# Two FP4 feed-forward stages with the residual added on TensorE, and retention's head-masked values copied instead of multiplied

## The chip, the cores and the metric

The kernel runs as one program on one core of a Trainium2 chip. The time is device microseconds from the start to the end of one execution; the kernel before was timed three times: 1815.0, 1809.85 and 1813.59 us, median 1813.59. The engines are TensorE (PE, with its weight loads as PEld), VectorE (DVE), ScalarE (ACT), GpSimd (POOL) and SyncE (SP), which only issues DMAs. They run their own instruction streams and meet at semaphores.

## The reference, cut to what matters

```python
x = L0_attn_x                                   # 4 x 1024 tokens of 128
x = x + 0.5 * _L0_ffn_ref(_layernorm(x), ...)   # mixture of 8 experts
x = x + _L0_attn_ref(_layernorm(x), ...)        # attention, 16 heads
x = x + 0.5 * _L0_ffn_ref(_layernorm(x), ...)
x = x + 0.5 * _L1_ffn_ref(_layernorm(x), ...)   # FP4 feed-forward (touched)
x = x + _L1_attn_ref(_layernorm(x), ...)        # retention, 16 heads of 8 (touched)
x = x + 0.5 * _L1_ffn_ref(_layernorm(x), ...)   # FP4 feed-forward (touched)

def fp4_quant_dequant(x):                       # blocks of 16 along the last dim
    scale = jnp.maximum(jnp.max(jnp.abs(xb), axis=-1, keepdims=True) / 6.0, 1e-12)
    xn = xb / scale
    idx = jnp.searchsorted(_MID, jnp.abs(xn))
    q = _GRID[idx] * jnp.sign(xn) * scale       # grid 0 .5 1 1.5 2 3 4 6

def _L1_ffn_ref(x, w_gate, w_up, w_down):       # 128 -> 352 -> 128
    gate = fp4_linear(x, w_gate)                # fp4_linear rewrites both operands
    y = fp4_linear(x, w_up)
    return fp4_linear(jax.nn.silu(gate) * y, w_down)

def _L1_attn_ref(x, Wq, Wk, Wv, gn_weight, gn_bias, Wout):
    scores = jnp.einsum('bhle,bhme->bhlm', Q, K) * Dm[None] / math.sqrt(HEAD_DIM)
    out = jnp.einsum('bhlm,bhme->bhle', scores, V)   # Dm: decay mask per head
    # group norm over each head's 8 channels and 1024 tokens, then @ Wout
```

Everything is fp32 here; "FP4" means values rounded to the grid and scaled back.

## The kernel before, in words

The tokens x (128 partitions, 32 tiles of 128 channels) stay in SBUF from first to last. Eight groups of four tiles go through each feed-forward stage. The stages follow one another, and each engine has its own code for each stage, written out in order by hand: what an engine does first is what stands first in its function, whether or not its input is there. In the trace the first FP4 stage (n = 3) runs from about 1400 to 1535 us, retention from there to about 1690, the second FP4 stage (n = 5) to the end at 1818.

**An FP4 group g.** VectorE rewrites the normalised tokens to codes (lines 1309 to 1317: block maximum, scale, reciprocal, product), ScalarE makes an "anchor" of them (line 1320, a bf16 power-of-two magnitude), VectorE rounds against it twice (1323, 1324) and scales back (1359). TensorE transposes the tokens (1541), ScalarE copies the transpose out of bank 6 (1495), and TensorE multiplies by gate and up (1551) into banks 0 to 5 in two pairs of tiles. ScalarE applies SiLU to a pair (1500), VectorE multiplies it with up (1432, `products`) into the hidden values, 128 x 1408. These go the same way: VectorE codes them (`ffn_codes`), ScalarE makes the anchor (`ffn_hidden_anchor`), VectorE rounds (`ffn_hidden_round`), GpSimd scales the codes back in one instruction of 1408 elements (1475, `ffn_pool`), TensorE transposes them in three chunks of columns (1566, `hiddenT`; chunks 0 and 2 in bank 6, chunk 1 in bank 7), ScalarE copies each chunk out (1490), TensorE multiplies by down (1574) into bank 7, and VectorE adds bank 7 to x (1438, `add`). The engines work on different groups at a time: in a turn TensorE does hiddenT(g-1), gate and up of g+1, down(g-1) and the tokens of g+2. In the first FP4 stage VectorE also takes the statistics of the finished sum (256) for the next normalisation, and GpSimd finishes them (271 to 282).

**Retention.** 32 chunks of 128 tokens, eight for each sequence. For a chunk TensorE projects q, k, v into a bank (1625 to 1627), ScalarE copies it (1723) and makes four masked copies of q (1726). TensorE takes scores of four groups of heads (1633), VectorE multiplies them with the decay (1802) and q and k with their decays (1797, 1798, the `masks`), and TensorE multiplies the decayed scores by `vm` (1643): the values, four times over (index j), with all channels at zero but those of the heads with number j in each group of four. GpSimd makes `vm` (1773) as a product of the values, repeated four times, with a constant mask of ones and zeros, 512 elements. It has two buffers, and is made when the outputs of two chunks before are done.

**Between the stages.** Each engine starts retention's first steps inside the FP4 stage, at `next(lead)`: ScalarE centres, scales and copies chunks 0 to 2 there, before the transposes of group 7, and TensorE takes the first score; the rest follows group 7.

## Time and profile before

| what | value |
|---|---|
| median of three runs | 1813.59 us (1809.85 to 1815.0) |
| the profiled execution | 1820.12 us, its span 1818.2 us |
| busy over the span | PE 1652.5 (91%), DVE 1406.3 (77%), ACT 990.2 (54%), POOL 345.9 (19%) |
| a group of the first FP4 stage, 1456.30 to 1470.50 | 14.20 us: PE 11.69, DVE 13.93, ACT 8.40, POOL 5.23, clock 0.88 |
| a group of the second FP4 stage, 1750.60 to 1764.40 | 13.80 us: PE 11.36, DVE 13.28, ACT 8.19, POOL 2.62, clock 0.88 |
| retention, 1530 to 1676 | 146 us: PE 138.0, DVE 135.9, ACT 82.1, POOL 64.2, clock 0.99 |

Busy time is per engine, and the engines work side by side, so the columns do not add up to the stretch. The clock is the mean of TensorE's granted clock, 1.00 being 2.4 GHz; it has two levels, 1.2 and 2.4 GHz, so 0.88 means a part of the stretch at the lower one. An instruction's start in the timeline is counted from the span's start. "Idle before <-releaser" is the time that the engine stood idle before an instruction and the instruction that ended it. The chain that ended last is followed back from the last instruction; in retention VectorE's line 1798 is on it twice with 1.36 us, at 1603.24 and at 1639.72, and the statistics of a group (line 256) have 0.86 us busy in VectorE's timeline of the first FP4 stage.

### The profile page before, as it was taken

To read this page: it belongs to the slowest core of one execution; us is meant where nothing else is said; L and a number is where in the kernel's file an instruction comes from. 1 tells how busy PE (TensorE), PEld (TensorE's weight loads), DVE (VectorE), ACT (ScalarE), POOL (GpSimd) and SP (SyncE) were. 2 spreads that over 40 slices of the span, in tenths; PEclk is the share of its full clock that TensorE was granted. 3 is DMA by queue.
4 is the path that set the end of the run, shared out by engine and by line. 5 is a ranking of instruction groups with operands and counts; after the bars stand their busy time and mean duration, and the time that the engine had idled before them with its cause. 6 is when DMAs were issued, how large, how long until landed. Compare 5 with 4: busy or idle time off the path is not lost.

```text
span 1818.2 us, 30155 instructions
## 1 busy us (share of the span) xinstructions
PE 1652.5 (91%) x10801; PEld 962.2 (53%) x10801; DVE 1406.3 (77%) x2337; ACT 990.2 (54%) x1958; POOL 345.9 (19%) x661
## 2 busy tenths in 40 slices
PE   6899999879999999999999889999998788998686
PEld 5788888721111111111111248788887566665575
DVE  5765555688999999999999247655577897999895
ACT  3223333337888888888888752322333455654452
POOL 5311002461000001000000221011001135244211
PEclk9899999988999999999999979999999888999888
DMA  3000000121010100011101001000000000000000
GB/s 129 1 1 0 0 0 18 53 87 37 27 32 28 37 22 22 22 37 29 32 27 24 7 7 53 1 0 0 0 1 1 1 1 1 2 2 2 1 24 24
DMA packets 25301, 35.91 MB, mean 20 GB/s; under 512 B 5808, under 2 KB 19696, under 8 KB 24672
## 3 DMA queue, kind: packets, MB, share of 16 engines
q1 hardware_dynamic: 25184, 34.38, 6.3%
q8 instruction: 70, 1.15, 0.3%
q14 instruction: 47, 0.39, 0.1%
HBM read 22.57 MB, written 8.78 MB: 17 GB/s over the span
## 4 chain that ended last, share of the span: by engine, by line
PE 75%; DVE 12%; ACT 5%; issue 4%; POOL 3%; DMA 0%; SPq 0%; ACTq 0%; POOLq 0%; DVEq 0%
PE PS L968 14%; PE PS L437 12%; PE PS L956 10%; PE PS L426 7%; PE PS L427 6%; PE PS L428 6%; PE PS L945 5%; DVE neg_half L1103 3%; ACT probs L1040 3%; PE PS L1551 3%; PE PS L1633 2%; PE PS L1566 2%; POOL qk_all L1475 2%; PE PS L1643 1%; DVE qk_all L1324 1%
## 5 line engine op out<-in xcount | busy, mean ns | idle before, releaser
L1103 DVE TENSOR_REDUCE neg_half<-PS 128x2 f32<-128x1024 f32 x512 | 601.5, 1220 | 39.7 <-PE PS L945 24.8
L1040 ACT ACTIVATE probs<-PS 128x512 f32<-128x512 f32 x1024 | 529.0, 603 | 118.7 <-PE PS L956 118.4
L520 ACT ACTIVATE shared<-PS 128x512 f32<-128x512 f32 x256 | 152.7, 597 | 376.8 <-PE PS L428 364.0
L956 PE MATMUL PS<-qk_all 51*128 51x512 bf16 x1024 | 282.0, 391 | 16.9 <-ACT probs L1040 11.8
L614 DVE TENSOR_TENSOR shared<-shared,PS 128x512 f32<-128x512 f32 x256 | 174.2, 686 | 158.1 <-ACT shared L520 156.2
L968 PE MATMUL PS<-probs,Vg 128*32 128x512 f32 x2048 | 279.1, 618 | 0.0
L437 PEld LDWEIGHTS PS<-wd,shared 128*128 128x128 f32 x2048 | 250.8, 194 | 11.2 <-issue 0.5
L956 PEld LDWEIGHTS PS<-qk_all 51*128 51x128 bf16 x1024 | 71.6, 93 | 340.8 <-ACT probs L1040 321.3
L437 PE MATMUL PS<-wd,shared 128*128 128x128 f32 x2048 | 252.0, 277 | 0.0
L945 PE MATMUL PS<-qk_all 48*128 48x512 bf16 x1024 | 194.4, 392 | 17.2 <-DVE neg_half L1103 15.0
L622 DVE SCALAR_TENSOR_TENSOR x<-PS,gates,x 128x128 f32 (+1 forms) x512 | 144.1, 344 | 73.2 <-PE PS L437 73.2
L426 PE MATMUL PS<-xT_hi,wg_hi 128*128 (+1 forms) x256 | 115.7, 452 | 9.8 <-DVE shared L614 8.5
L945 PEld LDWEIGHTS PS<-qk_all 48*128 48x128 bf16 x1024 | 49.6, 94 | 137.3 <-DVE neg_half L1103 132.1
L271 POOL TENSOR_TENSOR ln_a<-stats 128x4 f32<-128x4 f32 (+2 forms) x44 | 9.7, 221 | 536.7 <-DVE stats L256 536.5
L427 PE MATMUL PS<-xT_lo,wg_hi 128*128 (+1 forms) x256 | 102.9, 402 | 0.0
L427 PE MATMUL PS<-xT_lo,wu_hi 128*128 (+1 forms) x256 | 102.8, 402 | 0.0
L428 PE MATMUL PS<-xT_hi,wg_lo 128*128 (+1 forms) x256 | 102.7, 401 | 0.0
L426 PE MATMUL PS<-xT_hi,wu_hi 128*128 (+1 forms) x256 | 102.7, 401 | 0.0
L428 PE MATMUL PS<-xT_hi,wu_lo 128*128 (+1 forms) x256 | 101.7, 397 | 0.0
L1551 PE MATMUL PS<-wguT,plane 128*128 128x352 f32 (+4 forms) x384 | 95.2, 409 | 3.0 <-ACT plane L1495 2.3
L1566 PE MATMUL PS<-ident,qk_all 128*128 128x128 f32 (+1 forms) x192 | 43.5, 398 | 46.9 <-POOL qk_all L1475 41.0
L1551 PEld LDWEIGHTS PS<-wguT,plane 128*128 128x128 f32 x384 | 69.7, 214 | 23.4 <-issue 6.7
(210 smaller groups left out, 2108.9 us busy)
## 6 DMA issues: line engine op xcount, KB each, us to landing
split<-qk_all SPq DMA_DIRECT2D x16, 384.0 KB, 3.3
qk_all<-split SPq DMA_DIRECT2D x64, 96.0 KB
qk_all<-split SPq DMA_DIRECT2D x64, 64.0 KB
qk_all<-split SPq DMA_DIRECT2D x64, 32.0 KB
shared<-OTs SPq DMA_DIRECT2D x60, 32.0 KB
probs<-in_ret_const SPq DMA_DIRECT2D x1, 1538.5 KB, 6.8
qk_all<-negT SPq DMA_DIRECT2D x96, 4.0 KB, 1.7
SC<-inverse SPq DMA_DIRECT2D x3, 512.0 KB, 5.0
```

Of the source, the lines that this page charges most:

```text
L426: pe.matmul(bank(b), lhs_hi[:, w], hi, start=True, stop=False)
L427: pe.matmul(bank(b), lhs_hi[:, w], lo, start=False, stop=False)
L428: last = pe.matmul(bank(b), lhs_lo[:, w], hi, start=False, stop=True)
L437: last = pe.matmul(bank(4 + e % 2)[:, j * P:(j + 1) * P], h[:, FCH * (e % 2) + f, j * P:(j + 1) * P], wd[:, e * FCH + f, :], start=(f == 0 ...
L520: act.activation(sg[:, f, :], bank(f), ACT.Silu).then_inc(s["silu"], 1)
L614: dve.tensor_tensor(h[:, FCH * (e % 2) + f, :], sg[:, f, :], bank(2 + f), ALU.mult).then_inc(s["h"], 1)
L945: last = pe.matmul(bank(b + strip), qs[at, slot, 0, pair, t * P:(t + 1) * P], qs[at, slot, 1, pair, half * GW:(half + 1) * GW], start=True ...
L956: pe.matmul(bank(RING_AT + use % RING), qs[rows, slot, 1, pair, kt * P:(kt + 1) * P], qs[rows, slot, 0, pair, half * GW:(half + 1) * GW], ...
L968: last = pe.matmul(bank(7)[j * 32:(j + 1) * 32, :], Vg[:, r % 2, kt, j, :], probs[:, n % 2, j, :], start=(kt == 0), stop=(kt == BT - 1))
L1040: act.activation(probs[:, n % 2, STRIPS * strip + pair, :], bank(RING_AT + use % RING), ACT.Exp, scale=ATT_SCALE).then_inc(s["exped"], 1)
L1103: dve.tensor_reduce(neg_half[m % 2][:, i % 2, :, at], bank(use_bank(i, m), 2).rearrange("p (s w) -> p s w", s=STRIPS), AX.X, ALU.max, nega ...
L1551: last = pe.matmul(bank(3 * k, 3)[:, to:to + w], xqT[:, (2 * k + j) * P:(2 * k + j + 1) * P], wguT[:, src:src + w], start=True, stop=True)
```

## The change

Five edits. (1) VectorE's `add` goes; `down` begins each tile with a matmul of x by the identity, so that the sum arises in bank 7, and ScalarE copies bank 7 over x (`added`). (2) In ScalarE's turn the anchor of the hidden codes stands before both SiLUs instead of between them. (3) GpSimd scales the hidden codes back in two instructions of 704 elements, each with its own count on the semaphore, and TensorE's `hiddenT` transposes chunks 0 and 1 for the first two tiles, then for the other two, then chunk 2. (4) `vm` is cleared once (1024 elements) and then each chunk copies only the 128 values, 4 x 4 runs of 8, to their places. (5) The waits follow these.

```diff
@@ -179,7 +179,10 @@
         rxn = carve(2 * P).rearrange("p (u w) -> p u w", u=2)
         assert taken[0] <= HW
         qd, kd = (carve(3 * P).rearrange("p (u w) -> p u w", u=3) for _ in range(2))
-        vm = carve(2 * JH * P).rearrange("p (u j w) -> p u j w", u=2, j=JH)
+        vm_at, vm = taken[0], carve(2 * JH * P).rearrange("p (u j w) -> p u j w", u=2, j=JH)
+        HEAD_STEP = P + C // (HG * JH)
+        vm_heads = [space[:, vm_at + u * JH * P:vm_at + u * JH * P + JH * HEAD_STEP].rearrange("p (j w) -> p j w", w=HEAD_STEP)
+                    [:, :, 0:P].rearrange("p j (g e) -> p j g e", g=HG)[:, :, :, 0:C // (HG * JH)] for u in range(2)]
         rtmp, state = carve(P), carve(P)
         ro, cn = carve(2 * SEQ), carve(SEQ)
         rst = carve(12).rearrange("p (a k) -> p a k", k=3)
...
@@ -1366,7 +1369,7 @@
                 dve.wait_ge(ffn["xq"], done_groups(n) + tokens)
                 link.mark(q_largest(dve, fxn[:, tokens % 2, :], tmax))
             link(q_largest(dve, hraw, amax))
-            wait(dve, ffn["hq"], c)
+            wait(dve, ffn["hq"], PAIRS * c)
             if tokens < GROUPS:
                 q_inverse(dve, link, largest_all, scale_all)
                 q_codes(dve, fxn[:, tokens % 2, :], tcode, tmax, NB_T, ffn["t_raw"])
@@ -1432,11 +1435,6 @@
                     dve.tensor_tensor(hraw[:, k * PW:(k + 1) * PW], fsg[:, k, :], bank(3 * k, 3)[:, PW:2 * PW],
                                       ALU.mult).then_inc(s["h"], 1)
 
-            def add(g):
-                dve.wait_ge(s["y"], c0 + g + 1)
-                xs = x[:, g * GT:(g + 1) * GT, :].rearrange("p t c -> p (t c)")
-                dve.tensor_tensor(xs, bank(7), xs, ALU.add).then_inc(s["added"], 1)
-
             if n == 3:
                 ffn_tokens_round(dve, link, n, 0)
             for _ in ffn_tokens(dve, link, n, 1):
@@ -1449,19 +1447,16 @@
                 if g + 2 < GROUPS:
                     ffn_tokens_round(dve, link, n, g + 2)
                 ffn_hidden_round(dve, link, n, g)
-                if g > 0:
-                    add(g - 1)
                 if n == 3 and g > 1:
                     dve.wait_ge(s["added"], c0 + g - 1)
                     ln_stats(dve, g - 2)
             if n == 3:
                 dve.wait_ge(s["added"], c0 + GROUPS - 1)
                 ln_stats(dve, GROUPS - 2)
-                dve.wait_ge(s["hq"], GROUPS)
+                dve.wait_ge(s["hq"], PAIRS * GROUPS)
             next(lead, None)
-            add(GROUPS - 1)
-            dve.wait_ge(s["added"], c0 + GROUPS)
             if n == 3:
+                dve.wait_ge(s["added"], c0 + GROUPS)
                 ln_stats(dve, GROUPS - 1)
 
         def ffn_pool(pool, n, lead=iter(())):
@@ -1472,7 +1467,11 @@
                     ln_finish(pool, 4, g - 3)
                 pool.wait_ge(s["h_code"], c + 1)
                 wait(pool, s["hT_ps"], 3 * c)
-                pool.tensor_tensor(q_blocks(hq), q_blocks(hcode), q_wide(fscale, GT * NB_I), ALU.mult).then_inc(s["hq"], 1)
+                nb = GT * NB_I // 2
+                for k in range(PAIRS):
+                    half = slice(k * PW, (k + 1) * PW)
+                    pool.tensor_tensor(q_blocks(hq[:, half]), q_blocks(hcode[:, half]), q_wide(fscale[:, k * nb:(k + 1) * nb], nb),
+                                       ALU.mult).then_inc(s["hq"], 1)
             if n == 3:
                 for g in range(GROUPS - 3, GROUPS):
                     if g == GROUPS - 1:
@@ -1498,6 +1497,11 @@
                 act.wait_ge(s["gu"], (c0 + g) * PAIRS + k + 1)
                 wait(act, s["h"], (c0 + g - 1) * PAIRS + k + 1)
                 act.activation(fsg[:, k, :], bank(3 * k, 3)[:, 0:PW], ACT.Silu).then_inc(s["silu"], 1)
+
+            def added(g):
+                act.wait_ge(s["y"], c0 + g + 1)
+                xs = x[:, g * GT:(g + 1) * GT, :].rearrange("p t c -> p (t c)")
+                act.activation(xs, bank(7), ACT.Copy).then_inc(s["added"], 1)
 
             ffn_normalise(act, n, 1)
             ffn_tokens_anchor(act, n, 0)
@@ -1516,18 +1520,20 @@
                         hiddenT(g - 1, c)
                 if g + 2 < GROUPS:
                     ffn_tokens_anchor(act, n, g + 2)
-                if g + 1 < GROUPS:
-                    silu(g + 1, 0)
                 ffn_hidden_anchor(act, n, g)
                 if g + 1 < GROUPS:
-                    silu(g + 1, 1)
+                    for k in range(PAIRS):
+                        silu(g + 1, k)
                 if g + 3 < GROUPS:
                     ffn_normalise(act, n, g + 3)
+                if g > 0:
+                    added(g - 1)
                 if g + 2 < GROUPS:
                     tokensT(g + 2)
             next(lead, None)
             for c in range(len(CHUNKS)):
                 hiddenT(GROUPS - 1, c)
+            added(GROUPS - 1)
 
         def ffn_pe(pe, n, lead=iter(())):
             s = ffn
@@ -1552,27 +1558,35 @@
                                                  wguT[:, src:src + w], start=True, stop=True)
                     last.then_inc(s["gu"], 1)
 
-            def hiddenT(r, c):
-                lo, w = CHUNKS[c]
-                pe.wait_ge(s["hq"], c0 + r + 1)
-                if c == 0:
-                    pe.wait_ge(s["xT"], c0 + min(r + 3, GROUPS))
-                    wait(pe, s["hT"], 3 * (c0 + r))
-                elif c == 1:
-                    wait(pe, s["added"], c0 + r)
-                else:
-                    pe.wait_ge(s["hT"], 3 * (c0 + r) + 1)
-                for j in range(GT):
-                    last = pe.transpose(bank(6 + c % 2)[0:w, j * P:(j + 1) * P],
-                                        hq[:, j * INNER + lo:j * INNER + lo + w], ident[:, :])
-                last.then_inc(s["hT_ps"], 1)
+            def hiddenT(r):
+
+                def turned(c, pair):
+                    lo, w = CHUNKS[c]
+                    for j in (2 * pair, 2 * pair + 1):
+                        last = pe.transpose(bank(6 + c % 2)[0:w, j * P:(j + 1) * P],
+                                            hq[:, j * INNER + lo:j * INNER + lo + w], ident[:, :])
+                    return last
+
+                pe.wait_ge(s["hq"], PAIRS * (c0 + r) + 1)
+                pe.wait_ge(s["xT"], c0 + min(r + 3, GROUPS))
+                wait(pe, s["hT"], 3 * (c0 + r))
+                turned(0, 0)
+                wait(pe, s["added"], c0 + r)
+                turned(1, 0)
+                pe.wait_ge(s["hq"], PAIRS * (c0 + r + 1))
+                turned(0, 1).then_inc(s["hT_ps"], 1)
+                turned(1, 1).then_inc(s["hT_ps"], 1)
+                pe.wait_ge(s["hT"], 3 * (c0 + r) + 1)
+                turned(2, 0)
+                turned(2, 1).then_inc(s["hT_ps"], 1)
 
             def down(r):
                 pe.wait_ge(s["hT"], 3 * (c0 + r + 1))
                 for j in range(GT):
+                    pe.matmul(bank(7)[:, j * P:(j + 1) * P], ident[:, :], x[:, r * GT + j, :], start=True, stop=False)
                     for c, (lo, w) in enumerate(CHUNKS):
                         last = pe.matmul(bank(7)[:, j * P:(j + 1) * P], hqT[0:w, c, j * P:(j + 1) * P], wdT[0:w, c, :],
-                                         start=(c == 0), stop=(c == len(CHUNKS) - 1))
+                                         start=False, stop=(c == len(CHUNKS) - 1))
                 last.then_inc(s["y"], 1)
 
             tokens(0)
...
...
@@ -1768,10 +1780,12 @@
 
             for k in range(CHUNKS_ALL):
                 b, c = k // BT, k % BT
+                if k == 0:
+                    pool.memset(vm[:, :, :, :].rearrange("p u j w -> p (u j w)"), 0.0).then_inc(s["vm_zero"], 1)
+                    pool.wait_ge(s["vm_zero"], 1)
                 pool.wait_ge(s["pj"], k + 1)
                 wait(pool, s["o_ps"], k - 1)
-                pool.tensor_tensor(vm[:, k % 2, :, :], vs[:, k % 3, :].unsqueeze(1).to_broadcast([P, JH, C]), k_col,
-                                   ALU.mult).then_inc(s["vm"], 1)
+                pool.tensor_copy(vm_heads[k % 2], vs[:, k % 3, :].rearrange("p (g j d) -> p j g d", g=HG, j=JH)).then_inc(s["vm"], 1)
                 if k == 0:
                     yield
                 if b > 0 and c == 2:
```

ScalarE's turn for one group in the middle of the second half of the first FP4 stage. Names: qk_all and shared are areas in SBUF that hold the stage's buffers, PS is PSUM; L1320 of 128x1408 is the hidden anchor, L1500 a SiLU. Before:

```order
L1490 ACTIVATE qk_all<-PS 128x512 [waits ffn_y,ffn_hT_ps] x2
L1490 ACTIVATE qk_all<-PS 96x512 [waits ffn_y,ffn_hT_ps]
L1320 ACTIVATE qk_all<-qk_all 128x512 [waits ffn_t_raw]
L1500 ACTIVATE shared<-PS 128x704 [waits ffn_h,ffn_gu]
L1320 ACTIVATE qk_all<-qk_all 128x1408 [waits ffn_h_raw]
L1500 ACTIVATE shared<-PS 128x704 [waits ffn_h,ffn_gu]
L1393 ACTIVATE xn<-x,mean 128x128 [waits ln_rstd,ffn_t_raw]
L1393 ACTIVATE xn<-x,mean 128x128 x3
L1398 ACTIVATE xn<-xn,rstd 128x128 [waits ffn_centred]
L1398 ACTIVATE xn<-xn,rstd 128x128 x3
L1495 ACTIVATE plane<-PS 128x512 [waits ffn_gu,ffn_xT_ps]
```

Now (L1323 the anchors, L1499 the SiLUs, L1504 the copy of the sum to x):

```order
L1489 ACTIVATE qk_all<-PS 128x512 [waits ffn_y,ffn_hT_ps] x2
L1489 ACTIVATE qk_all<-PS 96x512 [waits ffn_y,ffn_hT_ps]
L1323 ACTIVATE qk_all<-qk_all 128x512 [waits ffn_t_raw]
L1323 ACTIVATE qk_all<-qk_all 128x1408 [waits ffn_h_raw]
L1499 ACTIVATE shared<-PS 128x704 [waits ffn_h,ffn_gu] x2
L1396 ACTIVATE xn<-x,mean 128x128 [waits ln_rstd,ffn_t_raw]
L1396 ACTIVATE xn<-x,mean 128x128 x3
L1401 ACTIVATE xn<-xn,rstd 128x128 [waits ffn_centred]
L1401 ACTIVATE xn<-xn,rstd 128x128 x3
L1504 ACTIVATE x<-PS 128x512 [waits ffn_y]
L1494 ACTIVATE plane<-PS 128x512 [waits ffn_gu,ffn_xT_ps]
```

The hidden anchor moved in front of both SiLUs, and one copy more stands between the normalisation and the copy of the transposed tokens.

TensorE, the transposes of the hidden values of one group and the first matmul of gate and up. Before:

```order
L1566 MATMUL PS<-ident,qk_all 128x128 [waits ffn_hT,ffn_xT,ffn_hq]
L1566 MATMUL PS<-ident,qk_all 128x128 x3
L1566 MATMUL PS<-ident,qk_all 128x128 [waits ffn_added,ffn_hq]
L1566 MATMUL PS<-ident,qk_all 128x128 x3
L1566 MATMUL PS<-ident,qk_all 96x128 [waits ffn_hT,ffn_hq]
L1566 MATMUL PS<-ident,qk_all 96x128 x3
L1551 MATMUL PS<-wguT,plane 128x352 [waits ffn_h,ffn_xT]
```

Now:

```order
L1566 MATMUL PS<-ident,qk_all 128x128 [waits ffn_hT,ffn_xT,ffn_hq]
L1566 MATMUL PS<-ident,qk_all 128x128
L1566 MATMUL PS<-ident,qk_all 128x128 [waits ffn_added]
L1566 MATMUL PS<-ident,qk_all 128x128
L1566 MATMUL PS<-ident,qk_all 128x128 [waits ffn_hq]
L1566 MATMUL PS<-ident,qk_all 128x128 x3
L1566 MATMUL PS<-ident,qk_all 96x128 [waits ffn_hT]
L1566 MATMUL PS<-ident,qk_all 96x128 x3
L1557 MATMUL PS<-wguT,plane 128x352 [waits ffn_h,ffn_xT]
```

The wait for the last part of the rewrite stands behind four transposes instead of before the first. Further on, where `down` had twelve matmuls for four tiles (L1574), it now has four of x and twelve of down (L1586, L1588).

ScalarE where the first FP4 stage ends and retention begins, with the middle left out. Before (L1711 and L1715 centre and scale retention's chunks, L1719 copies a transposed chunk, L1723 and L1726 are its projection, L1490 the chunks of group 7):

```order
L1320 ACTIVATE qk_all<-qk_all 128x1408 [waits ffn_h_raw]
L1711 ACTIVATE qk_all<-x,mean 128x128 [waits ln_rstd,ld_ret]
L1711 ACTIVATE qk_all<-x,mean 128x128
L1715 ACTIVATE qk_all<-qk_all,rstd 128x128 [waits ret_centred] x2
L1719 ACTIVATE qk_all<-PS 128x128 [waits ret_xT_ps]
...
L1490 ACTIVATE qk_all<-PS 128x512 [waits ffn_y,ffn_hT_ps] x2
L1490 ACTIVATE qk_all<-PS 96x512 [waits ffn_y,ffn_hT_ps]
L1723 ACTIVATE qk_all<-PS 128x512 [waits ret_proj]
L1726 ACTIVATE qk_all<-PS,probs 128x128 x4
L1719 ACTIVATE qk_all<-PS 128x128 [waits ret_xT_ps]
```

Now (the same are L1723, L1727, L1731, L1735 and L1738, L1489):

```order
L1323 ACTIVATE qk_all<-qk_all 128x1408 [waits ffn_h_raw]
L1504 ACTIVATE x<-PS 128x512 [waits ffn_y]
L1723 ACTIVATE qk_all<-x,mean 128x128 [waits ln_rstd,ld_ret]
L1723 ACTIVATE qk_all<-x,mean 128x128
L1727 ACTIVATE qk_all<-qk_all,rstd 128x128 [waits ret_centred] x2
L1731 ACTIVATE qk_all<-PS 128x128 [waits ret_xT_ps]
...
L1489 ACTIVATE qk_all<-PS 128x512 [waits ffn_y,ffn_hT_ps] x2
L1489 ACTIVATE qk_all<-PS 96x512 [waits ffn_y,ffn_hT_ps]
L1504 ACTIVATE x<-PS 128x512 [waits ffn_y]
L1735 ACTIVATE qk_all<-PS 128x512 [waits ret_proj]
L1738 ACTIVATE qk_all<-PS,probs 128x128 x4
L1731 ACTIVATE qk_all<-PS 128x128 [waits ret_xT_ps]
```

The copy of group 6's sum stands before the first centring, and that of group 7's sum before the projection of chunk 1; each waits for its down.

## Rows read from the trace of the kernel before

**Rows 1.** Chain that ended last, 1380 to 1818: start us, us, what, count

```profile
1427.22 2.60 POOL qk_all L1475
...
1514.29 2.60 POOL qk_all L1475
...
1708.66 2.60 POOL qk_all L1475
...
1791.73 2.60 POOL qk_all L1475
```

**Rows 2.** Timeline of VectorE, 1750 to 1765: start, us, engine, line [idle before <-releaser]

```profile
1750.46 0.68 DVE L1438 TENSOR_TENSOR x<-PS,x 128x512 f32<-128x512 f32 x1
...
1751.06 1.67 DVE L1432 TENSOR_TENSOR qk_all<-shared,PS 128x704 f32<-128x704 f32 x2
...
1757.08 1.62 DVE L1317 TENSOR_TENSOR qk_all<-qk_all 128x1408 f32<-128x1408 f32 x1
...
1761.00 1.63 DVE L1323 SCALAR_TENSOR_TENSOR qk_all<-qk_all 128x1408 f32<-128x1408 bf16 x1 [0.25 <-ACT qk_all L1320]
...
1764.20 0.68 DVE L1438 TENSOR_TENSOR x<-PS,x 128x512 f32<-128x512 f32 x1
```

**Rows 3.** Groups by line and shape, 1410 to 1525: busy us, mean ns, idle before

```profile
L1323 DVE SCALAR_TENSOR_TENSOR qk_all<-qk_all 128x1408 f32<-128x1408 bf16 x8 | 13.0, 1622 | 8.8 <-ACT qk_all L1320 8.8
```

**Rows 4.** Groups by line and shape, 1690 to 1818

```profile
L1323 DVE SCALAR_TENSOR_TENSOR qk_all<-qk_all 128x1408 f32<-128x1408 bf16 x8 | 13.0, 1625 | 7.7 <-ACT qk_all L1320 7.7
```

**Rows 5.** Timeline of all engines, 1750 to 1762

```profile
1753.27 2.96 PE L1566 MATMUL PS<-ident,qk_all 128*128 128x128 f32 x12 [2.44 <-POOL qk_all L1475]
...
1756.01 5.43 PE L1551 MATMUL PS<-wguT,plane 128*128 128x352 f32 x24
...
1759.60 1.37 ACT L1320 ACTIVATE qk_all<-qk_all 128x1408 bf16<-128x1408 f32 x1
...
1761.28 2.84 PE L1574 MATMUL PS<-wdT,qk_all 128*128 128x128 f32 x24
```

**Rows 6.** Stretches: us, PE, PEld, DVE, ACT, POOL busy, clock, DMA

```profile
1754.30:1755.30 1.00, 1.00 (x6) 0.70 (x5) 0.93 (x3) 0.63 (x2) 0.00 (x0) 0.50 0.00 0
...
1427.20:1442.20 15.00, 12.34 (x64) 10.30 (x64) 12.53 (x15) 7.16 (x15) 2.59 (x1) 0.72 0.00 0
```

**Rows 7.** Timeline of all engines, 1520 to 1537

```profile
1520.12 4.91 PE L1574 MATMUL PS<-wdT,qk_all 128*128 128x128 f32 x24 [0.68 <-ACT qk_all L1490]
...
1522.96 0.68 ACT L1711 ACTIVATE qk_all<-x,mean 128x128 f32<-128x128 f32 x2
...
1535.16 0.69 DVE L1438 TENSOR_TENSOR x<-PS,x 128x512 f32<-128x512 f32 x1 [3.14 <-PE PS L1574]
...
1536.78 1.14 PE L1633 MATMUL PS<-qk_all 32*128 32x512 f32 x8
```

**Rows 8.** One line each, 1797, 1798, 1802: ns min/median/max, first and last start

```profile
L1797 DVE TENSOR_TENSOR qk_all<-qk_all,probs x32: 274/292/1358, 1529.1 to 1666.5; 128x128 f32<-128x128 f32 x32
...
L1798 DVE TENSOR_TENSOR qk_all<-qk_all,probs x32: 277/284/1364, 1529.3 to 1666.7; 128x128 f32<-128x128 f32 x32
...
L1802 DVE TENSOR_TENSOR shared<-PS,probs x128: 667/679/693, 1529.5 to 1672.9; 128x512 f32<-128x512 f32 x128
```

**Rows 9.** VectorE's groups by line and shape, 1528 to 1690

```profile
L1797 DVE TENSOR_TENSOR qk_all<-qk_all,probs 128x128 f32<-128x128 f32 x32 | 12.9, 402 | 3.2 <-ACT qk_all L1723 2.1 <-POOL qk_all L1475 0.6
...
L1798 DVE TENSOR_TENSOR qk_all<-qk_all,probs 128x128 f32<-128x128 f32 x32 | 12.3, 384 | 0.0
```

**Rows 10.** GpSimd's groups by line and shape, whole span

```profile
L1773 POOL TENSOR_TENSOR qk_all<-qk_all,probs 128x512 f32<-128x512 f32 x32 | 41.1, 1289 | 39.5 <-PE PS L1649 36.6 <-PE PS L1643 2.4
...
L1157 POOL COPY Vg<-plane 128x256 f32<-128x256 f32 x16 | 6.4, 398 | 177.9 <-PE PS L968 177.8
...
L1151 POOL MEMSET Vg<- 128x512 f32 x2 | 1.1, 547 | 0.0
```

**Rows 11.** Timeline of all engines, 1807 to 1815

```profile
1809.48 5.28 PE L1574 MATMUL PS<-wdT,qk_all 128*128 128x128 f32 x24 [0.68 <-ACT qk_all L1490]
```

8 lines of the change are left out of this document (3 added, 5 removed).

## The prediction

> **What bounds the kernel now.** I read the chain that ended last first. In both FP4 stages it repeats itself once for each of the eight groups: GpSimd's rewrite of the hidden codes (line 1475), TensorE's transposes, half of gate and up, ScalarE's anchor, VectorE's two roundings, GpSimd again. The starts of line 1475 give the length of a group [rows 1]: six periods from 1427.22 to 1514.29 in the first stage, 87.07 us or 14.5 each, and six from 1708.66 to 1791.73 in the second, 83.07 us or 13.8 each.
>
> Then VectorE's timeline of one group [rows 2]. From one add to the next are 13.74 us (1750.46 to 1764.20); 0.60 of it is the add (the products start at 1751.06), 0.25 is a wait for ScalarE's anchor (line 1320), and the rest is work. So VectorE needs 12.89 us for a group, and the chain above is level with it. The groups by line say what that wait comes to [rows 3, 4]: 8.8 us before line 1323 in the first stage, 7.7 in the second.
>
> Then all engines in the same group [rows 5]. TensorE is idle for 2.44 us before the transposes, which take 2.96 us, gate and up take 5.43, down 2.84. The anchor starts at 1759.60 although its input, the codes, is ready at 1758.70 (1757.08 + 1.62, [rows 2]), since a SiLU that waits for gate and up stands in front of it. The clock table shows 0.50, the lower level of 1.2 GHz, in the microsecond from 1754.3 [rows 6]: it falls behind TensorE's idle time in each group, for about 3 us.
>
> Last, retention. VectorE and TensorE are both nearly full there, 3.7 us per chunk at best. Lines 1797 and 1798, products of two SBUF tensors, have medians of 292 and 284 ns but maxima of 1358 and 1364, while line 1802, which has one input in PSUM, stays within 667 and 693 in all 128 [rows 8]. Each long one lies under a product of GpSimd (line 1773, 1289 ns, [rows 10]). So VectorE is held there by GpSimd.
>
> **The change, part by part.**
>
> **FP4, the add leaves VectorE.** 0.60 us a group [rows 2]. The residual goes through TensorE as four more matmuls and is copied out by ScalarE. A matmul of this shape costs 2.84 / 24 = 0.118 us at full clock [rows 5] and 5.28 / 24 = 0.22 at half [rows 11], so 0.47 to 0.88 us a group on TensorE. ScalarE's copy of a bank takes what its copies of a bank take now, 0.60; ScalarE is busy for 8.2 of 13.8 us (the table of stretches), so both have cover while the add that they replace had none. Five adds lie between the first and the last of the seven rewrites of the first stage: 5 x 0.60 = 3.0. In the second I count to the eighth rewrite: 6 x 0.60 = 3.6.
>
> **FP4, the anchor goes ahead of both SiLUs.** What it waits for is then VectorE's own codes, and its 1.37 us [rows 5] lie under the token rounds, except in the last two groups of a stage, which have no token rounds: there some 1.44 us of wait remain (1.37 and the handing over). From [rows 3, 4]: 8.8 - 2 x 1.44 = 5.9, and 7.7 - 2.9 = 4.8. What is late next: the SiLUs. They end some 11 us into a group, and the products that need them come at 12.9, so they are hidden, save before the last group of the second stage, where a group without tokens is short: I take off 0.5.
>
> **FP4, the rewrite in two halves.** GpSimd pays its fixed cost of about 0.2 us twice: half of 2.6 becomes some 1.4 us, the second half ends 0.2 us later than the whole did, but half of eight transposes is done by then. Four transposes fewer behind it are 0.5 us at full clock and 0.9 at half. This makes gate and up begin 0.3 to 1.0 us sooner, which bounds nothing while VectorE does; I count 0.
> The Trainium skill (GPSIMD Engine Reference, "Elementwise — side-by-side cycle accounting") gives a two-input instruction about 2.6 cycles an element at 1.2 GHz. By that the 1408 elements would take an estimated 3.05 us where the row shows 2.60, and the halves would give the second one 0.2 us later still; the sum would be the same.
>
> **Does TensorE's own round then bind?** Its pieces at full clock: eight transposes 0.9, the copy that bank 6 waits for 0.9 with hand-over, four transposes 0.5, gate and up 5.1, down with 28 matmuls 3.1 to 3.3, tokens 0.5, and copy and hand-over of the tokens 1.2. That is 12.2 to 12.4, just under VectorE's 12.89. With 3 us at half clock, as now, 1.5 are added: 13.8, and VectorE would gain nothing in a group of the second stage. But idle time behind the tokens shrinks from 2.44 to about 1.2 us, so I expect the fall in few groups. I take 1.5 us off for it over both stages, with 0 and 5 as ends.
>
> FP4 sum: (3.0 + 5.9) + (3.6 + 4.8 - 0.5) - 1.5 = 15.3 us gained.
>
> **Entry to retention: ScalarE's queue.** The copy of the sixth sum (group 6 of 0 to 7) stands in front of retention's first centrings, and it waits for down, which ended at 1525.0 (1520.12 + 4.91, [rows 7]). Before, the centrings ran under it (1522.96). Now copy 0.60, two centrings 0.68 and two scalings 0.68 follow down: retention's first score comes up to 2.0 us later, and the transposes of group 7 queue behind it on TensorE. The same again one step on: group 7's copy waits for its down (its old add started at 1535.16) and holds up the projection of chunk 1, 0.60 + 0.60 + 1.14 = 2.3 us with what follows, 2.0 to 2.9 with hand-over, less what stood there; so the score at 1536.78 comes 2.0 to 5.7 us later against group 6. The gain of group 7 itself is already outside my count. GpSimd's new memset of 1024 elements, some 1.0 us by twice the 547 ns for 512 [rows 10], lies beside it. I take -4.0, nearer to both delays than to one.
>
> **Retention: 128 elements copied where 512 were multiplied.** GpSimd's copy of 256 elements takes 398 ns [rows 10], so I put one of 128 at 0.3 us, with 0.25 and 0.5 as ends, against 1.29. GpSimd itself has room; what counts is VectorE held behind it. Means less medians: (402 - 292) x 32 = 3.5 us and (384 - 284) x 32 = 3.2 [rows 8, 9], 6.7 together. Other instructions of two SBUF inputs are held now and then, so I put the whole at 7 to 9 us. A copy can hold for a quarter of that time and meets a two-input instruction less often. The floor is 0 (TensorE, at 3.7 us a chunk, might bind wherever VectorE is freed), the ceiling 9. Since the stalls are in chunks where VectorE is the longer of the two, I take 6.5.
> The Trainium skill (GPSIMD Engine Reference, "Specifications") says that GpSimd's SBUF interfaces are shared with VectorE and contended by its instructions with two SBUF inputs. By that rule the copy holds VectorE too, only for less; the trace agrees for the product (1364 against 284 ns), and no copy here shows it.
>
> **The end.** Behind the last rewrite 28 matmuls at half clock follow in place of 24 [rows 11]: +0.9; the second half of the rewrite +0.2; fewer transposes behind it -0.5 to -0.9, ScalarE's copy in place of the add -0.1. That is +0.1 to +0.5 lost; I take 0.4, since TensorE idles before it and will be at half clock.
>
> **Sum.** 15.3 - 4.0 + 6.5 - 0.4 = 17.4 us gained. The profiled execution took 1820.12 us (span 1818.2), so 1802.7 for one like it. It stands 6.5 us above the median of the runs, 1813.59, and they are what the prediction is about: 1813.6 - 17.4 = 1796.2, rounded to 1796.
>
> **Rivals.**
> *TensorE's round binds.* The clock keeps falling in every group, the round stays at 13.8. For it: the transposes now come in three bursts with gaps between them, and the clock fell after 2.44 us in each group. Against: gaps shorten. FP4 then gives about 7 less (its second stage and a part of the first): 1803. Chance 0.15.
> *Retention gives nothing and the entry costs all.* TensorE, busy 138 of 146 us there (the table of stretches), binds instead. For it: in chunks of 3.7 us it has no idle time. Against: two of the long ones, at 1603.24 and 1639.72, lie on the chain that ended last (told under the table of the profile). 17.4 - 6.5 - 1.7 = 9.2: 1804. Chance 0.12.
> *Slower: the lower clock spreads from the transposes to gate, up and down.* TensorE's round is 12.3 us and half of whatever is spent at 1.2 GHz; it passes 13.8 from 3 us on, and with 8 us at half clock it is 16.3. For it: the first period, with a mean clock of 0.72, lasted 15.0 us [rows 6]; the new order breaks the transposes in two. Thirteen periods at +2.2 to +2.5 are +30, less 6.5 in retention, and with the entry about +27: 1841; with 5 us at half clock +14 - 6.5 + 4 = +12: 1825. Chance 0.05.
> *Entry and tail eat it.* Ends of all terms against me at once, within 5 us of before: 1810. Chance 0.08.
> The forecast has the remaining 0.60.
>
> **How the numbers follow.** What a measurement can tell from no change is 0.3%, 5.4 us: faster is below 1808.2. The forecast and the first two rivals are faster, 0.87, of which I leave 0.02 to slower for what I did not see; no change 0.09; slower 0.06, with 0.85 for faster. Range: all ends for me are 15.3 + 1.5 - 2.0 + 9 = 24 us, 1790, and the runs before spread by 4 below their median: 1786. Upwards it takes in both faster rivals and stops at 1808.
>
> **What would show it.** Starts of the rewrite's first half some 12.9 us apart in the second stage and 13.7 in the first, where the statistics of a group, 0.86 busy, are added; no wait at all of the hidden rounding for the anchor but in the last two groups; a granted clock of 1.00 in most of the middle groups; ScalarE's copy ahead of retention's centrings with TensorE idle behind down; lines 1797 and 1798 with means below 320 ns and a copy near 0.3 us. I am wrong if the periods stay at 13.7 in the second stage (the round of TensorE), or the chunks of retention keep their 138 us with the stalls gone.

## The result, and the profile after

Six timed runs of the changed kernel have a median of 1797.09 us (1788.68 to 1801.45), six of the kernel before beside them 1812.55 us (1804.05 to 1816.41). The ratio is 0.9921, with a 95% interval of 0.9892 to 0.995: 15.5 us less between the medians, where 17.4 were forecast (1796.0 as the time). The profiled execution took 1800.72 us, its span is 1798.9.

I cut both spans at the same events: the starts of GpSimd's eight rewrites (T0 to T7 in the first FP4 stage, T0' to T7' in the second) and of the outputs of retention's first and last chunk (the first of a chunk's 32 matmuls of line 1643 before, 1655 after). A period is the time from one rewrite's start to the next; the entry is the stretch from T6 to the first outputs.

| from, to | before | after | difference | forecast |
|---|---|---|---|---|
| start, T0 (the same work) | 1427.2 | 1423.1 | -4.1 | 0 |
| T0, T6 | 87.07 | 79.00 | -8.1 | -8.9, less a part of the 1.5 |
| T6, first outputs | 23.57 | 32.28 | +8.7 | +4.0 |
| first, last outputs | 138.02 | 127.62 | -10.4 | -6.5 |
| last outputs, T0' | 32.78 | 35.01 | +2.2 | 0 |
| T0', T7' | 94.53 | 87.39 | -7.1 | -7.9, less the rest of the 1.5 |
| T7', end | 15.04 | 14.52 | -0.5 | +0.4 |

The stretches of the changed kernel, from rewrite to rewrite (columns as in [rows 6]):

```profile
1423.10:1435.81 12.71, 10.79 (x45) 8.27 (x46) 12.44 (x15) 5.41 (x9) 2.73 (x3) 0.67 0.00 0
1435.81:1449.64 13.83, 12.58 (x90) 10.97 (x90) 12.53 (x15) 10.36 (x24) 2.73 (x3) 1.00 0.00 1
1736.00:1748.80 12.80, 11.02 (x75) 9.18 (x74) 12.53 (x15) 8.62 (x18) 2.73 (x3) 1.00 0.00 0
1761.55:1772.40 10.85, 9.08 (x43) 6.82 (x43) 9.20 (x10) 4.90 (x7) 2.73 (x2) 0.84 0.00 1
1530.00:1662.00 132.00, 129.31 (x1613) 85.59 (x1614) 122.60 (x317) 78.95 (x269) 27.58 (x94) 0.99 0.01 2
```

A middle group of the second stage takes 12.80 us with VectorE busy for 12.53 and the clock at 1.00. Before it took 13.8 with the clock at 0.88. VectorE's wait for the hidden anchor, by line and shape in the first stage, 1410 to 1525 (the second stage has the same number):

```profile
L1326 DVE SCALAR_TENSOR_TENSOR qk_all<-qk_all 128x1408 f32<-128x1408 bf16 x8 | 13.0, 1619 | 3.4 <-ACT qk_all L1323 3.4
```

It was 8.8 and 7.7 [rows 3, 4]. TensorE's timeline of a middle group of the second stage:

```profile
1737.58 0.63 PE L1566 MATMUL PS<-ident,qk_all 128*128 128x128 f32 x4 [0.78 <-POOL qk_all L1473]
1738.73 0.66 PE L1566 MATMUL PS<-ident,qk_all 128*128 128x128 f32 x4 [0.53 <-POOL qk_all L1473]
1739.86 0.64 PE L1566 MATMUL PS<-ident,qk_all 128*96 128x128 f32 x4 [0.47 <-ACT qk_all L1489]
1740.34 5.25 PE L1557 MATMUL PS<-wguT,plane 128*128 128x352 f32 x24
```

In place of one wait of 2.44 us [rows 5] there are three, of 0.78, 0.53 and 0.47, and the clock stays up. In retention, one line each (ns min/median/max, first and last start):

```profile
L1811 DVE TENSOR_TENSOR qk_all<-qk_all,probs x32: 273/291/376, 1519.5 to 1653.7; 128x128 f32<-128x128 f32 x32
...
L1812 DVE TENSOR_TENSOR qk_all<-qk_all,probs x32: 275/284/372, 1519.7 to 1653.9; 128x128 f32<-128x128 f32 x32
...
L1788 POOL COPY qk_all<-qk_all x32: 289/293/406, 1524.5 to 1661.6; 128x128 f32<-128x128 f32 x32
...
L1784 POOL MEMSET qk_all<- x1: 951/951/951, 1523.5 to 1523.5; 128x1024 f32 x1
```

The maxima of 1358 and 1364 ns are gone [rows 8]. The entry to retention, on all engines:

```profile
1510.20 1.49 PE L1588 MATMUL PS<-wdT,qk_all 128*128 128x128 f32 x6
...
1513.52 0.83 PE L1588 MATMUL PS<-wdT,qk_all 128*128 128x128 f32 x6
...
1515.28 0.60 ACT L1504 ACTIVATE x<-PS 128x512 f32<-128x512 f32 x1 [4.29 <-PE PS L1588]
1515.77 0.68 ACT L1723 ACTIVATE qk_all<-x,mean 128x128 f32<-128x128 f32 x2
1516.36 0.68 ACT L1727 ACTIVATE qk_all<-qk_all,rstd 128x128 f32<-128x128 f32 x2
1516.89 0.53 PE L1632 MATMUL PS<-ident,qk_all 128*128 128x128 f32 x2 [1.65 <-ACT qk_all L1727]
```

ScalarE idles for 4.29 us before the copy of sum 6, and the centrings, which need nothing of it, stand behind; TensorE then idles for 1.65. Six matmuls of down take 1.49 us in the first of these rows and 0.83 in the second: down began at half clock (granted 0.50 from 1510.2 to 1511.6). Before, the centrings ran under down [rows 7].

### The profile page after: what moved, and what is told of

The parts are those of the page before. It is cut to its first block, busy times and chain, and to the rows that moved or that the text cites. A ratio compares the mean times of both kernels' runs of the same rounds, so it can differ in the third digit from the quotient of the medians.

```text
span 1798.9 us, 30396 instructions
## 1 busy us (share of the span) xinstructions
PE 1647.4 (92%) x10929; PEld 960.1 (53%) x10929; DVE 1387.4 (77%) x2321; ACT 997.3 (55%) x1974; POOL 317.0 (18%) x678
## 4 chain that ended last, share of the span: by engine, by line
PE 77%; DVE 11%; ACT 5%; issue 4%; POOL 2%; DMA 0%; SPq 0%; POOLq 0%; ACTq 0%; DVEq 0%
PE PS L971 14%; PE PS L440 12%; PE PS L959 10%; PE PS L429 7%; PE PS L430 6%; PE PS L431 6%; PE PS L948 5%; PE PS L1557 3%; DVE neg_half L1106 3%; ACT probs L1043 3%; PE PS L1645 2%; PE PS L1655 2%; PE PS L1588 1%; PE PS L329 1%; PE PS L1566 1%
## 5 line engine op out<-in xcount | busy, mean ns | idle before, releaser
L1816 DVE TENSOR_TENSOR shared<-PS,probs 128x512 f32<-128x512 f32 x128 | 79.3, 680 | 3.6 <-PE PS L1645 2.3
L1557 PEld LDWEIGHTS PS<-wguT,plane 128*128 128x128 f32 x384 | 69.6, 213 | 23.4 <-issue 6.3
```

The costliest lines, as they stand in the source:

```text
L1557: last = pe.matmul(bank(3 * k, 3)[:, to:to + w], xqT[:, (2 * k + j) * P:(2 * k + j + 1) * P], wguT[:, src:src + w], start=True, stop=True)
```

## The experiments

Each kernel was timed beside the kernel before on the same chip. The table has the ratio to it with its 95% interval, and cuts of the profiled execution.

| kernel | ratio | T0 to T6 | T6 to outputs | retention | T0' to T6' | T0 to end |
|---|---|---|---|---|---|---|
| before | 1 | 87.07 | 23.57 | 138.02 | 83.08 | 391.0 |
| changed | 0.9921 (0.9892 to 0.995) | 79.00 | 32.28 | 127.62 | 75.39 | 375.8 |
| 1 FP4 alone | 0.9949 (0.9928 to 0.997) | 79.05 | 27.62 | 138.15 | 75.24 | 381.0 |
| 2 copy alone | 0.9955 (0.9932 to 0.9978) | 87.15 | 23.57 | 127.68 | 82.78 | 380.8 |
| 3 product behind | 0.9908 (0.988 to 0.9937) | 79.00 | 27.62 | 132.48 | 75.87 | 375.0 |
| 4 sums by VectorE | 0.9879 (0.9849 to 0.9909) | 79.06 | 23.44 | 127.69 | 75.45 | 365.7 |
| 5 product ahead | 0.9935 (0.9914 to 0.9956) | 79.05 | 27.62 | 135.42 | 75.06 | 377.7 |
| 6 product after masks | 0.9936 (0.991 to 0.9961) | 79.02 | 27.60 | 135.19 | 75.19 | 377.6 |
| 7 copy ahead | 0.9905 (0.9872 to 0.9938) | 79.03 | 27.60 | 129.15 | 75.47 | 371.7 |
| 8 queue order | 0.9855 (0.9835 to 0.9874) | 79.02 | 27.38 | 127.64 | 75.19 | 370.8 |
| 9 anchor between | 0.9925 (0.9909 to 0.9941) | 81.09 | 29.92 | 127.68 | 79.67 | 379.0 |
| 10 add on VectorE | 0.9917 (0.9901 to 0.9934) | 83.24 | 26.69 | 127.65 | 80.24 | 377.8 |
| 11 rewrite whole | 0.9893 (0.987 to 0.9915) | 79.45 | 28.45 | 127.60 | 75.76 | 371.1 |
| 12 add, unused matmuls | 0.9953 (0.993 to 0.9977) | 86.05 | 25.81 | 127.62 | 84.89 | 385.2 |

T0 lies anywhere from 1413.8 to 1427.4 in these profiles, though the work before it is the same (only the anchor's place in the first group differs, and from the first gate and up to T0 all take 21.2 to 21.3 us); so profiles are compared by their cuts. A cut is of one execution. Stages that an edit does not touch repeat within 0.15 us in retention and mostly within 0.5 in the FP4 stages; the entry does not, as will be seen.

**1. The FP4 edits alone.**

```diff
-                pool.tensor_copy(vm_heads[k % 2], vs[:, k % 3, :].rearrange(...))
+                pool.tensor_tensor(vm[:, k % 2, :, :], vs[:, k % 3, :].unsqueeze(1).to_broadcast([P, JH, C]), k_col, ALU.mult)
```

> The FP4 edits alone; retention keeps its product of 512 columns. By the ledger of the two profiled executions the FP4 edits gave 8.1 + 7.7 us in their stages and cost about 8.7 + 2.2 us at the two borders of retention, so this kernel should stand only some 4 to 6 us below the one before (ratio 0.997 to 0.998), with retention's 32 chunks from the first outputs to the last at 138 us as before, the means of the two products of SBUF tensors at about 400 and 384 ns, and both FP4 stages 7.5 to 8 us shorter from first to last rewrite. If the loss behind the first FP4 stage belongs to the new copy in retention (its memset of 951 ns, its wait) and not to the FP4 edits, the border is back at 23.6 us here and the ratio is 0.993. If part of retention's gain came from the FP4 stages (the clock at its start, say), its chunks are below 138 us here.

Retention was back at 138.15 us, and both FP4 stages kept their gain. The entry was neither of the two numbers: 27.62, so 4.05 longer than before and not 8.7. The ratio, 0.9949, is accordingly below the 0.997 to 0.998 expected, which had 8.7 us in it. **2. The copy alone**, put into the kernel before:

> The copy of 128 elements alone, in the kernel before. My theory: retention's chunks go from 138 to 127.5 us by this edit alone, nothing else moves: 10 to 10.5 us less, ratio 0.9943. If the copy only pays beside the FP4 edits, or if the entry to retention pays for it (memset), the ratio is 0.997 or more. The two ratios of this and of the FP4 edits alone should multiply to that of the whole change, 0.992.

Retention took 127.68 us, all of the gain, and nothing else moved. So the two halves of the change are independent; 0.9949 x 0.9955 = 0.9904, inside the interval of the whole.

**3. GpSimd busy behind the copy.**

```diff
                 pool.tensor_copy(vm_heads[k % 2], ...)
+                wait(pool, s["busy"], k)
+                pool.tensor_tensor(scratch[:, k % 2, :, :], k_col, k_col, ALU.mult).then_inc(s["busy"], 1)
```

> The changed kernel, and behind each copy of 128 elements GpSimd multiplies 512 constants by themselves into a buffer that nobody reads: work added, result unused. TensorE gets its values as early as in the changed kernel, but GpSimd again runs a product with two SBUF inputs of 512 elements in each of the 32 chunks. Theory (VectorE is held while GpSimd's product runs): the long instructions on VectorE come back (maxima near 1360 ns, excess 7 to 9 us), retention goes from 127.6 back to 136 to 138 us, ratio to the kernel before 0.997 to 0.999. Rival (the product was late for TensorE, which had to wait for it): retention stays within 1 us of 127.6 and the ratio is 0.992, whether VectorE's instructions are long or not.

Neither: 132.48, about half of the way back. I call it a hold when a VectorE instruction takes longer than it does alone because it waits for GpSimd's. The timeline at the end of the second sequence (GpSimd and VectorE):

```profile
1593.43 0.38 POOL L1789 COPY qk_all<-qk_all 128x128 f32<-128x128 f32 x1
1593.58 0.38 DVE L1814 TENSOR_TENSOR qk_all<-qk_all,probs 128x128 f32<-128x128 f32 x1
1593.78 1.08 POOL L1791 TENSOR_TENSOR scratch<-probs 128x512 f32<-128x512 f32 x1
1593.88 1.12 DVE L1815 TENSOR_TENSOR qk_all<-qk_all,probs 128x128 f32<-128x128 f32 x1
```

VectorE's second product ends 0.15 us behind GpSimd's, after 1.12 us in place of 0.28. A second kind of instruction is held too, a product of four elements in the statistics of a sequence, which takes 0.17 us alone:

```profile
1599.75 1.04 POOL L1791 TENSOR_TENSOR scratch<-probs 128x512 f32<-128x512 f32 x1
1599.80 1.01 DVE L1831 TENSOR_TENSOR qk_all<-qk_all 128x4 f32<-128x4 f32 x1
```

In the kernel before both of a pair were held at such a place:

```profile
1600.73 1.02 POOL L282 TENSOR_TENSOR rstd<-ln_c,minus_half 128x4 f32<-128x4 f32 x1
1601.83 2.63 POOL L1773 TENSOR_TENSOR qk_all<-qk_all,probs 128x512 f32<-128x512 f32 x2
1601.96 1.36 DVE L1797 TENSOR_TENSOR qk_all<-qk_all,probs 128x128 f32<-128x128 f32 x1
1603.24 1.36 DVE L1798 TENSOR_TENSOR qk_all<-qk_all,probs 128x128 f32<-128x128 f32 x1
```

This also says why the pair is rarely held (two here, two 36 us later, three others in 32 chunks): in most chunks GpSimd's product waits for outputs and starts when VectorE's pair is done; only where GpSimd's queue is late, behind line 282 or once line 1767, do the two meet. The products of four elements (lines 1814 and 1816) are held three times more. The Trainium skill (SBUF — State Buffer, "SBUF: two separate sides") calls the port pair that GpSimd and VectorE share a lock, held for the whole instruction, for which a VectorE instruction with two SBUF inputs waits; the trace agrees (1.12 beside 1.08 us).

The intervals between the starts of outputs tell what is lost where. The table has the changed kernel's interval, how much longer that of the others is, and in brackets how much longer VectorE's held instructions in it are than alone (us; the intervals left out are the same in all within 0.02):

| outputs of chunks | changed | before | 3 | 5 | 7 |
|---|---|---|---|---|---|
| 0 to 8 | 29.78 | 1.19 (1.8) | 0.00 (0) | 0.00 (0) | 0.00 (0) |
| 8 to 11 | 12.94 | 3.40 (2.1) | 0.01 (0) | 4.23 (1.2) | 0.31 (0.4) |
| 13 to 18 | 21.49 | 2.39 (2.6) | 1.62 (1.7) | 1.17 (1.3) | 0.32 (0.4) |
| 21 to 26 | 21.49 | 2.40 (2.6) | 3.20 (1.7) | 1.36 (1.5) | 0.33 (0.4) |
| 29 to 31 | 8.01 | 1.01 (0.3) | 0.02 (0) | 1.02 (0) | 0.56 (0) |

In most rows the loss is what the holds add to VectorE, within 0.2 us (in the first the kernel before loses 0.6 less). Two things are not. In the last row run 5 loses 1.02 us without a hold; there GpSimd's values come late, and the outputs of chunk 31 start 0.10 us after its copy ends. The values are as late for chunks 15 and 23, but the rows 13 to 18 and 21 to 26 show no loss from it beyond the holds. And three intervals lose 1.3 to 3.1 us more than their holds; TensorE's clock fell in each. In the kernel before it begins with a held instruction of four elements (0.16 us alone):

```profile
1570.08 1.26 POOL L1773 TENSOR_TENSOR qk_all<-qk_all,probs 128x512 f32<-128x512 f32 x1 [2.08 <-PE PS L1643]
1570.12 1.24 DVE L1816 SCALAR_TENSOR_TENSOR qk_all<-qk_all 128x4 f32<-128x4 f32 x1
...
1572.31 2.82 PE L1633 MATMUL PS<-qk_all 32*128 32x512 f32 x8 [1.00 <-DVE shared L1802]
```

TensorE idles for 1.00 us behind it and is then at half clock. In the kernel before and in the changed one, from 1.24 to 3.24 us behind the start of chunk 9's outputs:

```profile
1576.30:1578.30 2.00, 2.00 (x16) 1.71 (x9) 0.67 (x3) 0.57 (x2) 0.00 (x0) 0.50 0.00 0
```

```profile
1570.65:1572.65 2.00, 2.00 (x17) 1.64 (x20) 1.76 (x9) 0.94 (x3) 0.05 (x1) 1.00 0.00 0
```

The granted clock is 0.50 in run 5 too, from 1558.5 to 1561.5, and in run 3 from 1641 to 1643. So of the 10.4 us some 9.4 are holds and the clock that fell behind them, and 1.0 is late values.

**5, 6 and 7. The same product ahead of the copy; product and copy behind VectorE's pair; a copy of 512 ahead.**

```diff
+                wait(pool, s["busy"], k)
+                pool.wait_ge(s["masked"], k + 1)                                      # 6 only
+                pool.tensor_tensor(scratch[:, k % 2, :, :], k_col, k_col, ALU.mult)   # 7: tensor_copy(..., k_col)
                 pool.tensor_copy(vm_heads[k % 2], ...)
```

> The changed kernel, with GpSimd's product of 512 constants (result unused) ahead of the copy of 128 elements in each chunk, so that it starts when the product of the kernel before started and the values come about as late as then, or 0.3 us later. The run with the product behind the copy lost 4.9 of retention's 10.4 us and had VectorE's long instructions in 3 places. If a hold of VectorE that starts together with the product is the whole cause, all 7 us of excess over the medians come back here (pairs of 1.1 to 1.36 us near chunks 10, 14 and 24) and retention takes 136 to 139 us; ratio to the kernel before 0.997 to 0.998. If most of the gain is that TensorE gets its values earlier, retention is above 138 us whatever VectorE shows.

135.42 us: the values are late again, and of the holds three long ones return, instructions of 1.13, 1.13 and 0.98 us. Retention falls just short of the range expected, and the ratio is lower still.

> The changed kernel, with GpSimd's product of 512 constants (result unused) and the copy behind it put after VectorE's two products of SBUF tensors in each chunk: GpSimd works as long as in the run before this one and the values come later still (some 1.8 us behind the projection), but the two products of VectorE can't be held. If the hold is the cause: no long instructions at lines of the two products, excess under 0.5 us, retention 127.6 to 129 us, ratio 0.992. If lateness of the values is the cause: retention 134 us or more, ratio 0.996 or above, with TensorE waiting for the copy.

This one did not tell the two apart. It gave 135.19 us and the same starts as run 5 nearly throughout: the wait was almost always over, and the product of one chunk met VectorE's pair of the next. A kernel with late values and no hold was not made; what late values cost by themselves is read from the row 29 to 31 above.

> As the first of these, but with a copy of 512 constants (one SBUF input, result unused) in place of the product, ahead of the copy of 128. If any instruction of GpSimd holds VectorE's products for as long as it runs, retention loses in proportion to its time, which I estimate at 0.6 to 0.8 us from 398 ns for 256 elements: excess of 2 to 4 us, retention 130 to 133. If only two-input products hold it, the excess stays under 0.8 us (VectorE's instructions lengthen by the 0.085 us seen in the changed kernel) and retention under 129 us.

129.15 us with an excess of 0.8, both at the bound of the second theory; but the timeline decides for the first:

```profile
1582.10 0.71 POOL L1790 COPY scratch<-probs 128x512 f32<-128x512 f32 x1
1582.26 0.70 DVE L1814 TENSOR_TENSOR qk_all<-qk_all,probs 128x128 f32<-128x128 f32 x1
```

A copy holds VectorE too, to its own end: 0.70 us in place of 0.29 (the page named above speaks of any GpSimd instruction that reads SBUF, and the trace agrees). By the table it costs no more than its holds and, in the last row, its lateness. What changed with the copy of 128 is the time it holds, and how late GpSimd is.

**4. The last two sums copied by VectorE.**

```diff
 def added(g):                                   # ScalarE
+    if g >= GROUPS - 2: return
...
+            added(GROUPS - 2)                    # VectorE: tensor_copy(xs, bank(7))
             next(lead, None)
+            added(GROUPS - 1)
```

> The changed kernel, except that the sums of the last two groups of each FP4 stage are copied out by VectorE, which idles there, in place of ScalarE; the residual still goes through TensorE. If ScalarE's queue is what the entry to retention pays (copy of sum 6 ahead of the first centrings, copy of sum 7 ahead of the projection of chunk 1), the way from the seventh rewrite to the first outputs of retention falls from 32.3 us to 27 to 29, and the ratio goes from 0.992 to about 0.990. If it is TensorE that is late there (its gate and up of the last group, transposes and down at half clock, 4 more matmuls each), it stays above 31 us and the ratio at 0.992.

The entry took 23.44 us, against 27.62 with the same 11.63 us from T6 to T7: all 4.2 us of it were ScalarE's queue. **8. ScalarE's queue in another order**, each engine doing the same work:

```diff
-                if g > 0:
+                if 0 < g < GROUPS - 1:
                     added(g - 1)
...
             next(lead, None)
+            added(GROUPS - 2)
+            next(lead, None)
             for c in range(len(CHUNKS)):
                 hiddenT(GROUPS - 1, c)
+            next(lead, None)
             added(GROUPS - 1)
...
             scale(1)
+            yield
             turned(0)
...
             turned(2)
+            yield
             centre(4)
```

> The changed kernel with ScalarE's queue alone in another order at the end of an FP4 stage: retention's first centrings and scalings ahead of the copy of sum 6, its projection of chunk 1 and the transposes' copy ahead of the copy of sum 7. All three engines do the same work. With the copies on VectorE the way from the seventh rewrite to retention's first outputs fell to 23.4 us, against 27.6 in two runs with them on ScalarE. If the place in ScalarE's queue is all of it, this order gives 23.5 to 24.5 us and a ratio of 0.988 to 0.989. If ScalarE's time itself (two copies of 0.6 us) or TensorE's queue (transposes of group 7 behind retention's first score) is what counts, it stays at 26 to 28 us and the ratio at 0.990 to 0.992.

27.38 us is in the range of the rivals, but in this execution TensorE was at half clock for a part of the way to T7, as in the changed kernel's own: from T5 to T6 the clock is 0.71 in both and 1.00 in runs 1, 3, 5, 6 and 7, the down of sum 6 ends 13.1 us after T6 in both and 9.1 after it in those. The changed kernel's took 32.28 us. With the same clock the order gives 4.9 us, as the sums on VectorE gave 4.2. The timeline shows the copy of sum 6 now behind the centrings:

```profile
1503.10 1.49 PE L1591 MATMUL PS<-wdT,qk_all 128*128 128x128 f32 x6
1503.78 0.68 ACT L1726 ACTIVATE qk_all<-x,mean 128x128 f32<-128x128 f32 x2
1504.37 0.68 ACT L1730 ACTIVATE qk_all<-qk_all,rstd 128x128 f32<-128x128 f32 x2
...
1508.17 0.60 ACT L1504 ACTIVATE x<-PS 128x512 f32<-128x512 f32 x1 [3.12 <-PE PS L1591]
```

Its ratio, 0.9855, is below the interval of the changed kernel: this version beats both.

**9, 10 and 11. The parts of the FP4 edit, each put back.**

```diff
+                if g + 1 < GROUPS: silu(g + 1, 0)         # 9
                 ffn_hidden_anchor(act, n, g)
...
+                    add(g - 1)                            # 10: VectorE, as before; no identity matmuls
...
+                pool.tensor_tensor(q_blocks(hq), q_blocks(hcode), q_wide(fscale, GT * NB_I), ALU.mult)   # 11
```

> The changed kernel, with ScalarE's anchor of the hidden codes put back between the two SiLUs, everything else as changed. My account gives the anchor's place 5.9 + 4.8 us of the FP4 stages' 15.7. If it holds, VectorE waits again before line 1326 in each group: periods of the second stage 12.80 + about 0.75 = 13.5, of the first 13.6 + 0.8 = 14.4, the two stages together 9 to 11 us longer than in the changed kernel (from 79.0 and 75.4 us) and the ratio to the kernel before about 0.998. If TensorE's round had been the true limit, or the SiLU no longer stands in the way because the groups are shorter, the periods stay within 0.3 us.

The stages got longer by 2.1 and 4.3 us up to T6, 6.4 together, not 9 to 11: some periods stay at 12.80, others go to 14.2 to 14.8. The entry took 29.92 us, 2.3 more than the 27.6 of runs 1, 3, 5, 6 and 7.

> The changed kernel, with the residual added by VectorE again in the FP4 stages and no identity matmuls on TensorE: the anchor's place, the halves of the rewrite and retention's copy stay. My account: the add is 0.60 us in each group, 3.0 + 3.6 us: periods 13.4 in the second stage and 14.2 in the first, and 4 us come back at the entry to retention since ScalarE has no copies in its queue (23.4 us from the seventh rewrite to the first outputs). Sum about +6.6 - 4.2 to -8.8: ratio 0.989 to 0.993, level with the changed kernel. Rival (the saved time was hidden behind TensorE's round): periods stay at 12.8 and the ratio is 0.988 or less.

Here it is 4.2 + 4.9 = 9.1 us, where 6.6 were expected, and the entry took 26.69 us, not 23.4. VectorE's add, by line and shape, 1420 to 1525:

```profile
L1441 DVE TENSOR_TENSOR x<-PS,x 128x512 f32<-128x512 f32 x7 | 4.8, 687 | 5.0 <-PE PS L1592 4.9
```

The add of a middle group waited for nothing in the kernel before (0.25 us of wait in the group shown are the anchor's, [rows 2]); with the anchor's wait gone it waits for TensorE's down. Of the 4.9 us, 2.0 lie between T0 and T6 and 2.9 in one wait behind T6, at the entry; from T0' to T6' it waits 2.2. So moving the add takes 0.60 us of work out of a group and this wait with it.

> The changed kernel, with GpSimd's rewrite as one instruction of 1408 elements in each group; TensorE keeps its new order of transposes, all of which now wait for the whole. I counted the halves at nothing while VectorE binds: middle periods stay at 12.80 and 13.6. Rival (the halves are what keeps TensorE's idle time short and its clock up): idle time before the transposes grows by 1.1 us, the clock falls to the lower level in each group, TensorE's round becomes the limit and periods go to 13.3 to 13.8, ratio 0.996 or more. In the short last groups of a stage (10.85 and 12.0 us), where the chain through GpSimd binds, I expect 0.3 to 1.0 us each lost: 1 to 3 us in all, ratio 0.993.

79.45 and 75.76 us: the halves are worth 0.4 us in each stage up to T6 and, with 28.45 at the entry, some 0.8 there; middle periods stay at 12.80 and the clock at 1.00. The ratio, 0.9893, does not show a loss. The ratios of runs 9 and 10, 0.9925 and 0.9917, lie inside the interval of the changed kernel too: what each part is worth rests on the cuts of one execution each.

**12. Unused matmuls.** A kernel like 10, with the four identity matmuls beside:

```diff
                 for j in range(GT):
+                    pe.matmul(bank(7)[:, j * P:(j + 1) * P], ident[:, :], x[:, r * GT + j, :], start=True, stop=True)
```

> The kernel of the run with the residual added on VectorE again, plus the four identity matmuls of the residual on TensorE, whose result is overwritten and not used: VectorE and ScalarE do what they did there, TensorE does 0.47 us more in each group. In that run the periods were 15.52, 14.23, 14.38, 14.18 and 14.78, 13.40, 14.02, 13.40 us, with a mean granted clock of 0.75 to 0.88 in part of them and 3.46 us of idle time on TensorE before the transposes of one. Theory A (the matmuls also fill TensorE's idle time and so keep its clock): the clock of the middle groups is 1.00, the periods are even at 13.40 in the second stage and 14.2 in the first, the two stages 2 to 4 us shorter than in that run (83.24 and 80.24 us); the price of the add alone is then 0.60 us a group. Theory B (the uneven periods come from VectorE's add or its waits): the same periods within 0.2 us. Theory C (TensorE's round binds there): 0.5 us more a group.

Theory A, which was mine, fell: periods of 12.75, 16.43, 13.40, 14.73, 13.40 and 14.19 us, the two stages 2.8 and 4.7 longer than in run 10, the nearest to theory C. The add's wait in the first stage (eight adds; the line of run 10 has seven):

```profile
L1441 DVE TENSOR_TENSOR x<-PS,x 128x512 f32<-128x512 f32 x8 | 5.5, 687 | 9.1 <-PE PS L1593 9.1
```

4.9 of the 9.1 us lie between T0 and T6, where run 10 has 2.0, and 6.8 between T0' and T6', where it has 2.2: the differences are what the stages got longer. More work on TensorE ends down later, and VectorE's whole queue stands behind the add. The matmuls don't keep the clock (0.75 to 0.88 in four of the ten middle periods); in the changed kernel they cost nothing because nothing on VectorE waits for down in a middle group.

## Why the prediction was right

**What bounds.** Right: periods of 12.80 us were forecast as 12.9, those with statistics 13.6 as 13.7, the clock 1.00 in the middle groups, the anchor's wait only at a stage's end (3.4 us where 2.9 were counted). TensorE's round, the first rival, did not bind; its idle time before the transposes is 1.8 us in three pieces, where 1.2 was expected.

**The FP4 sum.** 15.3 us forecast; from T0 to T6 and T0' to T7' it was 8.1 + 7.1 = 15.2. The split between its terms was wrong: add 6.6 and anchor 10.7 in the working, but 9.1 to 9.4 and 6.4 to 6.7 by runs 9 and 10 (each term once taken from the changed kernel, once from the one before; the first six periods of each stage; the larger number of each has the halves in it). The idle time in front of line 1323 hid another wait behind it, that of the add for down, so the anchor's price was some 4 us too high and the add's 2.5 to 2.8 too low; the 2.0 taken off for the clock and the SiLUs, of which the middle groups show nothing, made up most of the rest. That the sum came out is luck in part. The halves were counted at 0 and are 0.8 in both stages; that the second ends 0.2 us later than the whole did is right (2 x 1.386 against 2.588).

**The entry.** Mechanism and size right: -4.0 forecast, 4.05 in the runs with the clock up there, and ScalarE's order shown as the cause by runs 4 and 8. The profiled execution lost 8.7, since TensorE was at half clock before T7; I had no term for that, nor for the 2.2 us before the second FP4 stage, where the first gate and up began at half clock (7.27 us for 24 matmuls, 5.32 before). Neither shows in every execution: of the runs with the same FP4 code (1, 3, 5, 6 and 7) none had the first, and in them the second stretch took 32.5 to 34.6 us, where the changed kernel's took 35.0 and that of the kernel before 32.8. Why the clock is down in some of them and not in others, no run shows.

**Retention.** Right in kind, short in size: 6.5 forecast, 10.4 measured, and within 0.1 us the same in every run that has the copy and nothing beside it. I counted VectorE's excess over the medians in two lines (6.7), put the whole at 7 to 9, and took less. The held instructions add up to some 9 us, 1.9 of them in the products of four elements; with the clock behind them they cost 9.4, so taking less than the 7 to 9 was wrong. The ceiling of 9 was passed by two things: a hold can idle TensorE, and its clock was at half behind that; and GpSimd's latency, which had no term: 1.29 us against 0.29 on the way to the very last outputs, 1.0 us. That the copy holds VectorE "only for less" held: at most 376 ns for 291.

**The end.** 0.4 us lost were forecast, 0.5 gained in this execution, but from T7' on runs with the same code took 14.5 to 16.1 us; that term is smaller than this spread, and not shown.

**The sum.** 17.4 forecast, 15.5 in the medians, 15.2 in the cuts from T0 on (391.0 - 375.8), where retention's extra 3.9 us and the 0.9 of the end stand against the losses at half clock at retention's two borders (4.7 + 2.2). The total was near for that reason in part, and that is luck.

## What to carry to other kernels

Idle time before an instruction prices a wait only until the next wait in the same queue: before taking an edit at the idle time it removes, look at what the engine's next instructions wait for, and how long after. Work moved to an engine with idle time cost nothing here in the middle of a stage, and its full waiting at the stage's end, where unrelated work is queued behind it; there, putting the independent work first gave back the 4 to 5 us that the entry had cost. A GpSimd instruction that reads SBUF and that VectorE can meet should be short, whether it copies or multiplies; by these runs whom it holds (9.4 us with the clock) mattered more than who waits for its result (1.0 us), and an instruction of four elements can be the one that is held.

## What the runs showed that was not expected

- A plain copy on GpSimd (512 elements, 0.71 us) held a VectorE product of two SBUF tensors, which took 0.70 us in place of 0.29; VectorE's product with one input in PSUM (line 1816 of the changed kernel) stayed within 666 to 693 ns in all 128 cases, and within 1 ns of that in runs 3, 5 and 7.
- A held VectorE product of 128x128 ended 0.14 to 0.15 us behind GpSimd's instruction each time, a held one of 128x4 0.02 us behind it, in the kernel before as in runs 1, 3, 5 and 7.
- The last group of the second stage, T6' to T7', took 12.00 us in some executions and 10.86 in others of the same FP4 code (runs 5 and 7).
- Up to T0 the same work took 1413.8 to 1427.4 us, a spread nearly as large as the effect that was measured.
